# A two-expert-layer macaron block on one core: expert weights turned one at a time, 64-row keys, the subtraction of maxima between the two halves of the scores, key and query loads one per slot

## The chip, the cores and the metric

One core of a Trainium2 chip runs the whole block; the other cores are idle. The metric is the device time of one execution in microseconds (us). The kernel before takes 968.02 us, the median of three runs (967.27 to 972.53). The engines are named as in the profile: PE is TensorE (PEld its weight loads), DVE VectorE, ACT ScalarE, POOL GpSimd, SP SyncE.

## What is computed

The input is 16 sequences of 256 tokens with 128 features, 4096 tokens in all. The block is an expert layer, an attention layer, and the same expert layer again:

```
x = x + 0.5 * experts(layernorm(x))
x = x + attention(layernorm(x))
x = x + 0.5 * experts(layernorm(x))

experts:   scores = softmax(xf @ gate_w.T)                 # 8 experts
           vals, idx = top_k(scores.T, 512)                # each expert takes its 512 best tokens
           y   = layernorm(xf[idx]) * ln_w + ln_b
           h   = gelu(y @ fc1.T + b1)                      # 128 -> 512
           out = (h @ fc2.T + b2) * vals                   # 512 -> 128
           xf  = xf.at[idx].add(out)
attention: 16 heads of 8, causal, s[q,k] = (Q.K + Q.pek[k-q]) / sqrt(8)
           out = softmax(s) @ V + sum_k softmax(s) pev[k-q];  then @ Wo.T
```

All weights and activations are float32. The scores are computed with bfloat16 matmuls on float32 numbers split into three bfloat16 parts; six products of parts (TERMS) are kept, and stand as 48 rows of the contraction (6 terms times 8 features). The relative scores need a second set of 48 rows, so that a query operand has 96 rows, and 32 more for the causal mask.

## The kernel before

The program is written by hand, engine by engine, with semaphores.

**Expert layer** (`expert_layer(n)`, n = 0, 1). After gating and a bit search for the 512th score, PE and DVE work out the token numbers of each expert (`passed_of`, `index_of`, L884 to L897). POOL fetches each expert's rows with four indirect DMAs (`gather`, L543), adds each expert's output into the result in DRAM with four more (`scatter`, L554), and each scatter waits until the one before has landed. Five experts' rows (AHEAD) are fetched ahead; after the scatter of e comes the gather of e + 5. In layer 0 the scatters of experts 3 to 6 are each followed by two memsets (L570, L571), which clear rows 32 to 127 of the key buffers for the attention. PE first turns all 16 weight blocks of the eight experts (L913; ACT copies each from one of two PSUM banks, L700 and L702). Then for each expert it turns the fetched rows (`turn_rows`, L920), DVE scales them (`rows_in`, L1308), PE does the first matmuls (`first_half`, L929), ACT the gelu (L710), PE the second (`second_half`, L939), DVE scales the output (`scale`, L1296), POOL scatters. The second half of an expert stands behind the first half of the next one. The order of PE's loop is

```
turn all weights; turn_rows(0)
for e: first_half(e); turn_rows(e + 1); second_half(e - 1)      # the last two: second_half(e) as well
```

**Parts.** The attention starts with projections (L973) in 16 pieces of 512 tokens, queries and keys in turn. ACT takes the first part (L726) and the second (L730), DVE and POOL (L591, L594) the rests; SP stores every piece to DRAM (L440, `query_parts` 768 KB, `key_parts` 384 KB) from one of four buffers. From piece 4 on, SP issues one of the nine loads of the first pair behind each store (L447).

**Attention by pairs.** Two sequences are a pair; eight pairs follow each other, the six in the middle in a loop on every engine that is run three times with two pairs in it. A pair has 12 slots, and a slot makes 2 x 16 x 32 columns of scores in two halves (u = 0, 1). Each half has 16 matmuls with the relative table (L1002) and 16 with the keys (L1005, 128 rows of which 48 hold keys and the rest zeros). Between the halves PE turns the partial maxima of the slot before (L1017). After the second half it subtracts the maxima of the slot two back by 16 matmuls (`subtract_maxima`, L1025), which releases that slot's exponential on ACT (L778, 128 x 1024). Then comes a piece (`chunk`, L1056 or L1066) of the output products of earlier slots. Scores live in three pairs of banks, so the scores of slot s + 1 wait for the exponential of s - 2.

SP loads the operands of the next pair at the start of a pair: nine DMAs (`stacked`, L469), 384, 256 or 128 KB each, 2304 KB in all. The parts that a term needs are chosen by the tables Q_PART and K_PART: a query load reads one part and repeats it three times (or twice), a key load reads consecutive parts. Behind them in SP's queue stand the stores of the head outputs (L453, four small DMAs each) and of the relative outputs (L457).

## Time and profile before

| | us |
|---|---|
| median of three runs | 968.02 |
| the profiled execution | 967.66 |
| its span, first to last instruction | 965.9 |
| expert layer 0 | 0 to 228 |
| parts, until the first scores | 228 to 312 |
| attention by pairs | 312 to 715 |
| output projection, expert layer 1 | 715 to 965.9 |

Busy shares of the span: PE 66%, PEld 53%, DVE 52%, ACT 31%, POOL 24%. These are averages over stages with different limits. A row of the trace gives start and length in us (or a length alone), engine, line and operation, the tiles (almost everything lies in one tile, `arena`), and in brackets the idle time before with what ended it.

### The profile page before, as it was taken

The numbers are of one execution on the slowest core, as the hardware profiler recorded it, in microseconds if no ns is written. First come the engines' busy times: TensorE is split into PE (matmuls) and PEld (weight loads), VectorE is DVE, ScalarE is ACT, GpSimd is POOL, SyncE is SP. The second block draws the span as 40 slices with busy tenths as digits, with TensorE's granted clock in tenths as the row PEclk, the third lists the DMA queues.
The fourth block names the chain that finished last, engine by engine and source line by source line (L and its number), as shares of the span: only waits on it lengthen the run. The fifth ranks groups of instructions, "written<-read, shape, count | busy, mean of one in ns | idle before, by whom it ended". The sixth has DMA issues, their size and how long they took to land.

```text
span 965.9 us, 29195 instructions
## 1 busy us (share of the span) xinstructions
PE 636.5 (66%) x12366; PEld 516.7 (53%) x12366; DVE 504.7 (52%) x1712; ACT 297.2 (31%) x473; POOL 235.6 (24%) x227
## 2 busy tenths in 40 slices
PE   4512998700733789888898879899972811689640
PEld 3501556500422678777787768788862800357430
DVE  7977222123721567565666557667766777512120
ACT  2390454300522232323232313232332264063210
POOL 2000738884533000000000000014110000346864
PEclk9999999955885599999898979999985555599985
DMA  4272213325355332323222323234342506112322
GB/s 122 59 218 80 53 17 43 34 24 142 132 160 173 92 62 70 59 69 60 69 44 74 52 70 56 65 72 97 75 110 46 175 1 178 24 35 31 45 25 22
DMA packets 99163, 73.27 MB, mean 76 GB/s; under 512 B 26569, under 2 KB 92258, under 8 KB 98914
## 3 DMA queue, kind: packets, MB, share of 16 engines
q1 hardware_dynamic: 85858, 57.01, 23.4%
q0 software_dynamic: 13184, 14.43, 9.2%
q8 instruction: 102, 1.67, 0.8%
q14 instruction: 19, 0.16, 0.1%
HBM read 44.34 MB, written 27.01 MB: 74 GB/s over the span
## 4 chain that ended last, share of the span: by engine, by line
PE 38%; DVE 15%; POOL 14%; issue 11%; ACT 9%; SPq 6%; DMA 5%; DVEq 0%; ACTq 0%; POOLq 0%
PE banks L1002 10%; ACT arena L778 8%; PE banks L1005 7%; POOL x_mid L554 5%; PE banks L1025 5%; POOL out_dram L554 5%; SPq L469 3%; DVE arena L1119 3%; PE banks L1066 2%; PE banks L849 2%; POOL arena L543 2%; PE banks L929 2%; PE banks L913 1%; DMA out_dram<-arena 1%; SPq L440 1%
## 5 line engine op out<-in xcount | busy, mean ns | idle before, releaser
L778 ACT ACTIVATE arena<-banks 128x1024 f32<-128x1024 f32 x96 | 98.3, 1024 | 263.4 <-PE banks L1025 263.4
L1002 PE MATMUL banks<-arena 128*128 128x32 bf16 x3072 | 126.8, 194 | 42.8 <-issue 16.1
L1002 PEld LDWEIGHTS banks<-arena 128*128 128x128 bf16 x3072 | 112.4, 101 | 68.1 <-ACT arena L778 38.7
L1366 DVE TRANSPOSE_TENSOR_REDUCE arena<-banks 128x32 f32<-128x1024 f32 x96 | 120.0, 1250 | 18.1 <-PE banks L1005 13.8
L1005 PE MATMUL banks<-arena 128*128 128x32 bf16 x3072 | 108.6, 178 | 8.6 <-issue 8.6
L1005 PEld LDWEIGHTS banks<-arena 128*128 128x128 bf16 x3072 | 93.6, 97 | 11.3 <-issue 11.3
L543 POOL DMA_INDIRECT arena<-table,arena x64 | 61.5, 961 | 126.2 <-DVE arena L1276 107.7
L607 POOL COPY arena<-arena 128x576 f32 (+1 forms) x8 | 5.3, 668 | 329.6 <-PE banks L1056 329.6
L1382 DVE TENSOR_REDUCE arena<-banks 32x8 f32<-32x64 f32 (+1 forms) x96 | 20.1, 209 | 107.9 <-PE banks L1017 107.8
L710 ACT ACTIVATE arena<-banks,arena 128x512 f32<-128x512 f32 x64 | 44.0, 687 | 85.2 <-PE banks L929 85.2
L1025 PE MATMUL banks<-arena 128*128 128x64 bf16 x1536 | 64.4, 198 | 0.7 <-issue 0.7
L929 PE MATMUL banks<-arena 128*128 128x512 f32 x128 | 61.0, 609 | 3.6 <-DVE arena L1308 3.6
L939 PE MATMUL banks<-arena 128*128 128x128 f32 x512 | 61.8, 281 | 1.6 <-ACT arena L710 1.6
L939 PEld LDWEIGHTS banks<-arena 128*128 128x128 f32 x512 | 60.6, 198 | 3.2 <-ACT arena L710 3.2
L554 POOL DMA_INDIRECT out_dram<-arena x32 | 50.2, 1568 | 33.6 <-DVE arena L1296 15.1
L871 PE MATMUL banks<-arena 128*128 128x1 bf16 x60 | 11.2, 186 | 71.4 <-DVE arena L1228 71.4
L1066 PE MATMUL banks<-arena 128*32 128x128 f32 x1536 | 56.4, 288 | 1.4 <-issue 1.2
L554 POOL DMA_INDIRECT x_mid<-arena x32 | 50.2, 1570 | 24.2 <-DVE arena L1296 14.8
L1025 PEld LDWEIGHTS banks<-arena 128*128 128x128 bf16 x1536 | 54.5, 101 | 1.0 <-issue 1.0
L1056 PE MATMUL banks<-arena 128*9 128x128 f32 x1536 | 52.4, 278 | 3.5 <-ACT arena L785 1.9
L1293 DVE TENSOR_TENSOR arena<-banks,arena 128x512 f32<-128x512 f32 x16 | 11.1, 692 | 82.0 <-DMA x_mid<-arena 33.6
L1308 DVE TENSOR_SCALAR arena<-banks,arena 128x512 f32<-128x512 f32 x16 | 13.0, 810 | 73.1 <-PE banks L920 73.1
(182 smaller groups left out, 1021.4 us busy)
## 6 DMA issues: line engine op xcount, KB each, us to landing
query_parts<-arena SPq DMA_DIRECT2D x8, 768.0 KB, 6.4
arena<-query_parts SPq DMA_DIRECT2D x16, 384.0 KB
table<-arena SPq DMA_DIRECT2D x2, 2176.0 KB, 9.4
arena<-in_L_ffn_fc2s_dram SPq DMA_DIRECT2D x4, 1024.0 KB, 10.8
arena<-query_parts SPq DMA_DIRECT2D x16, 256.0 KB
key_parts<-arena SPq DMA_DIRECT2D x8, 384.0 KB, 7.0
arena<-key_parts SPq DMA_DIRECT2D x8, 384.0 KB
head_outputs<-arena SPq DMA_DIRECT2D x128, 18.0 KB
```

The lines of the kernel that those rows point to most:

```text
L543: pool.indirect_dma_start(out=rows[:, s, :], out_offset=None, in_=table[n], in_offset=bass.IndirectOffsetOnAxis(ap=idx[:, s:s + 1], axis=0 ...
L554: pool.indirect_dma_start(out=total[n], out_offset=bass.IndirectOffsetOnAxis(ap=idx[:, s:s + 1], axis=0), in_=osb[:, e % 2, j, :], in_offs ...
L710: nc.scalar.activation(hT[:, e % 2, c, :], psum[:, H_B[k % 2], :], ACT.Gelu_apprx_tanh, bias=b1T[:, e * NC + c:e * NC + c + 1]).then_inc(s ...
L778: nc.scalar.activation(dst, psum[:, 2 * r:2 * r + 2, :].rearrange("p u (h n) -> p u h n", h=H), ACT.Exp, scale=HD ** -0.5).then_inc(s_prob, 1)
L929: pe.matmul(psum[:, H_B[k % 2], :], w1T[:, e, P * c:P * c + P], yT[:, e % 2, :], start=True, stop=True).then_inc(s_h, 1)
L939: last = pe.matmul(o, hT[:, e % 2, c, P * j:P * j + P], w2T[:, e, c, :], start=(c == 0), stop=(c == NC - 1))
L1002: pe.matmul(sc[:, :, 2 * a:2 * a + 2], rel_k[:, y:y + P], q_st[:, r, :, q0 + 2 * a:q0 + 2 * a + 2], start=(a == 0), stop=False, skip_group ...
L1005: last = pe.matmul(sc[:, h], k_st[:, r, h, L * b + P * kb:L * b + P * kb + P], q_st[:, r, h, q0:q0 + 32], start=False, stop=False, skip_gr ...
L1025: last = pe.matmul(psum[:, 2 * (s % 3) + u, 64 * g:64 * g + 64], m_wts[:, s % 3, col:col + 1].to_broadcast([P, P]), eye2, start=False, sto ...
L1056: end = pe.matmul(psum[32 * j:32 * j + HD + 1, bank, P * u:P * u + P], v_pair[:, buffer, 2 * batch + kb, 4 * u + j, :], probs[:, blk, H * ...
L1066: end = pe.matmul(psum[32 * j:32 * j + 32, bank, P * u:P * u + P], rel_v[:, HD * x:HD * x + 32], probs[:, blk, :, q0:q0 + 4], start=(kb == ...
L1366: step(v.tensor_reduce(mp, psum[:, 2 * (s % 3):2 * (s % 3) + 2, :].rearrange("p u (h n) -> p (u h) n", n=32), AX.X, ALU.max, apply_transpo ...
```

## The change

- **Expert weights.** PE turns the two weight blocks of expert e + 1 between the first and the second half of expert e; only expert 0's come first. ACT copies them behind the gelu of e. The second half of e follows in the same step. DVE's loop is `rows_in(e + 1); scale(e)`. The copies that set the parity rows of the queries (eight, on ACT) come after the last expert.
- **POOL.** AHEAD is 4, and the memsets are gone.
- **Keys.** Their matmuls use rows 0 to 63. DVE clears rows 32 to 63 of the key buffers once, at the start of the attention (one memset of 32 x 8192 words).
- **Slot.** The subtraction of slot s - 2 stands between the halves of slot s.
- **Loads.** The terms are renumbered, so that query loads read consecutive parts too; key parts are stored in reverse order. The loads of the next pair are issued one per slot, each behind the wait for that slot's scores, among the stores. In the loop the parts are kept as the outer dimension of the access; only the first pair's loads fold parts and features into one by hand. In the program as built both are the same: the distance of two parts is that of 128 rows of 4096 elements, and the source is one dimension of 384 (256, 128) rows with such a step. Before, the repeated part had a step of 0 and stayed a dimension of 3 (or 2) of its own.

```diff
-        Q_PART = (0, 0, 0, 1, 1, 2)
-        K_PART = (0, 1, 2, 0, 1, 0)
+        Q_PART = (0, 1, 2, 0, 1, 0)
+        K_PART = (2, 1, 0, 1, 0, 0)
...
-                    q = qs[c, Q_PART[a], 0:HD, :, bass.ds(pr * PT, PT)]
-                    q = q.unsqueeze(0).to_broadcast([b - a, HD, H, PT])
-                    k = ks[0:b - a, :, :, bass.ds(pr * PT, PT)].rearrange("w d h n -> (w d) h n")
+                    q = qs[c, 0:b - a, :, :, bass.ds(pr * PT, PT)]
+                    k = ks[3 - (b - a):3, :, :, bass.ds(pr * PT, PT)]
+                    if spread:
+                        q, k = (x.rearrange("w d h n -> (w d) h n") for x in (q, k))
...
-                    elif not last:
-                        sp.wait_ge(s_score, NS * pr)
-                    if not last:
-                        for dst, src in stacked(pr + 1, 1 - r):
-                            sp.dma_start(dst, src).then_inc(s_load[1 - r], 16)
+                    loads = [] if last else list(stacked(pr + 1, 1 - r, False))
+
+                    def load_in(slots):
+                        for s in slots:
+                            if loads:
+                                sp.wait_ge(s_score, NS * pr + s + 1)
+                                sp.dma_start(*loads.pop(0)).then_inc(s_load[1 - r], 16)
+
+                    load_in((0, 1))
                     if not first:
                         store_heads(AV_LATER0, pr - 1, 2 * pr - 2, 1)
+                    load_in((2, 3, 4, 5, 6))
+                    if not first:
                         store_relative(pr - 1)
+                    load_in((7, 8))
+                    if not first:
                         store_heads(AV_LATER1, pr, 2 * pr - 1, 1)
...
-                AHEAD = 5
+                AHEAD = 4
...
-                    elif n == 0 and e < E - 1:
-                        q, i = 2 * H // 4, e - (E - AHEAD)
-                        pool.memset(k_words[32:64, q * i:q * i + q], 0.0).then_inc(s_zero, 1)
-                        pool.memset(k_words[64:P, q * i:q * i + q], 0.0).then_inc(s_zero, 1)
-                        pool.wait_ge(s_zero, 2 * i + 2)
...
+                def turn_weights(e):
+                    for w in range(2):
+                        if w and e:
+                            pe.wait_ge(s_yT, n * E + e)
+                        else:
+                            pe.wait_ge(s_trf, weights_read(n, 2 * e))
+                        bank = tr_bank(tr + NXB + 3 * e + w)
+                        for c in range(NC):
+                            src = raw2[:, e, P * c:P * c + P] if w else raw1[:, e, c, :]
+                            last = pe.transpose(bank[:, P * c:P * c + P], src, ident)
+                        last.then_inc(s_tr, 1)
...
+                turn_weights(0)
                 turn_rows(0)
                 for e in range(E):
                     first_half(e)
                     if e + 1 < E:
+                        turn_weights(e + 1)
                         turn_rows(e + 1)
-
-                    if 0 < e < E - 1:
-                        second_half(e - 1)
-                    if e >= E - 2:
-                        second_half(e)
+                    second_half(e)
...
-                            last = pe.matmul(sc[:, h], k_st[:, r, h, L * b + P * kb:L * b + P * kb + P],
-                                             q_st[:, r, h, q0:q0 + 32],
+                            last = pe.matmul(sc[:, h], k_st[0:64, r, h, L * b + P * kb:L * b + P * kb + P],
+                                             q_st[0:64, r, h, q0:q0 + 32],
...
+                        if u == 0 and between:
+                            subtract_maxima(s - 2, pr)
...
-                        if s >= 2 or not first:
-                            subtract_maxima(s - 2, pr)
...
+                dve.wait_ge(s_tab, 16)
+                v.memset(k_words[32:64], 0.0).then_inc(s_zero, 1)
```

PE's order at the start of an expert layer, before. L913 turns weights, L920 rows, L929 is a first half, L939 a second:

```order
L913 MATMUL banks<-arena 128x128 x64
L920 MATMUL banks<-arena 128x128 x4
L929 MATMUL banks<-arena 128x512 x4
L920 MATMUL banks<-arena 128x128 x4
L929 MATMUL banks<-arena 128x512 x4
L920 MATMUL banks<-arena 128x128 x4
L939 MATMUL banks<-arena 128x128 x16
```

The same place after the change. L926 turns weights, L934 rows, L943 is a first half, L953 a second:

```order
L926 MATMUL banks<-arena 128x128 x8
L934 MATMUL banks<-arena 128x128 x4
L943 MATMUL banks<-arena 128x512 x4
L926 MATMUL banks<-arena 128x128 x8
L934 MATMUL banks<-arena 128x128 x4
L953 MATMUL banks<-arena 128x128 x16
L943 MATMUL banks<-arena 128x512 x4
```

56 of 64 turns have moved behind the first half of expert 0, and its second half is ahead of the first half of expert 1.

PE in one slot of the loop, before (L1002 relative, L1005 keys, L1017 maxima turned, L1025 subtraction, L1066 chunk):

```order
L1002 MATMUL banks<-arena 128x16x2 x16
L1005 MATMUL banks<-arena 128x32 x16
L1014 REGISTER_ALU
L1017 MATMUL banks<-arena 32x128
L1002 MATMUL banks<-arena 128x16x2 x16
L1005 MATMUL banks<-arena 128x32 x16
L1025 MATMUL banks<-arena 128x64 x16
L1045 ISA
L1066 MATMUL banks<-arena 32x128 x16
```

The same slot after the change (L1014 relative, L1017 keys, L1031 maxima turned, L1039 subtraction, L1080 chunk):

```order
L1014 MATMUL banks<-arena 128x16x2 x16
L1017 MATMUL banks<-arena 128x32 x16
L1028 REGISTER_ALU
L1031 MATMUL banks<-arena 32x128
L1039 MATMUL banks<-arena 128x64 x16
L1014 MATMUL banks<-arena 128x16x2 x16
L1017 MATMUL banks<-arena 128x32 x16
L1059 REGISTER_ALU
L1080 MATMUL banks<-arena 32x128 x16
```

Half of the scores now stands behind the subtraction. Nothing was added or taken away in the slot.

## Rows read from the trace of the kernel before

**Rows 1.** The chain that ended last: start, length, scatters 0, 3, 7 of both layers.

```profile
136.24 1.64 POOL x_mid L554
...
174.12 1.63 POOL x_mid L554
...
218.72 1.56 POOL x_mid L554
...
873.37 1.63 POOL out_dram L554
...
911.23 1.63 POOL out_dram L554
...
950.14 1.55 POOL out_dram L554
```

**Rows 2.** PE's timeline at the start of expert layer 0.

```profile
107.49 3.35 PE L913 MATMUL banks<-arena 128*128 128x128 f32 x16
...
119.14 0.63 PE L920 MATMUL banks<-arena 128*128 128x128 f32 x4 [0.28 <-ACT arena L700]
120.67 3.89 PE L929 MATMUL banks<-arena 128*128 128x512 f32 x8 [0.90 <-DVE arena L1308]
...
130.06 3.74 PE L939 MATMUL banks<-arena 128*128 128x128 f32 x32
```

**Rows 3.** The waits: us in total, times, longest.

```profile
PEld banks L1002 <- ACT arena L778: 38.7, 81, 2.6
...
DVE arena L1119 <- DMA arena<-x_mid: 23.2, 1, 23.2
...
PE banks L1002 <- issue: 16.1, 6, 3.6
```

**Rows 4.** ACT's timeline while parts are made: pieces 0, 8 and 9.

```profile
246.73 0.58 ACT L726 CAST arena<-banks 128x512 bf16<-128x512 f32 x1 [1.12 <-PE banks L973]
...
265.75 0.58 ACT L726 CAST arena<-banks 128x512 bf16<-128x512 f32 x1 [0.22 <-DMA query_parts<-arena]
275.56 0.59 ACT L726 CAST arena<-banks 128x512 bf16<-128x512 f32 x1 [9.22 <-DMA key_parts<-arena]
```

**Rows 5.** PE's timeline: the first scores, and the scores of slot 4.

```profile
311.92 0.65 PE L1002 MATMUL banks<-arena 128*128 128x32 bf16 x16 [9.08 <-DMA arena<-query_parts]
...
326.99 0.67 PE L1002 MATMUL banks<-arena 128*128 128x32 bf16 x16 [1.11 <-ACT arena L778]
```

**Rows 6.** SP's timeline: loads of a pair.

```profile
504.72 0.83 SPq L469 DMA_DIRECT2D arena<-query_parts  x1
...
559.50 9.79 SPq L469 DMA_DIRECT2D arena<-query_parts  x2
```

**Rows 7.** Windows: length, busy of PE, PEld, DVE, ACT, POOL; clock, DMA share, GB/s.

```profile
286.00:292.00 6.00, 1.25 (x2) 0.30 (x2) 0.69 (x1) 2.20 (x5) 3.28 (x3) 0.65 0.97 236
...
370.00:376.00 6.00, 5.89 (x200) 5.50 (x200) 5.17 (x13) 1.52 (x2) 0.00 (x0) 1.00 0.35 89
```

**Rows 8.** The timeline of one slot of the loop.

```profile
521.64 0.66 PE L1002 MATMUL banks<-arena 128*128 128x32 bf16 x16 [0.19 <-ACT arena L778]
...
524.10 1.08 PE L1066 MATMUL banks<-arena 128*32 128x128 f32 x32
...
525.28 0.54 PEld L1002 LDWEIGHTS banks<-arena 128*128 128x128 bf16 x16 [0.37 <-ACT arena L778]
```

**Rows 9.** PE's timeline: a 128-row matmul, then two of 32 rows.

```profile
94.21 0.19 PE L895 MATMUL banks<-arena 128*128 128x1 bf16 x1
94.33 0.21 PE L897 MATMUL banks<-arena 32*128 32x1 bf16 x2
```

**Rows 10.** The chain again: an idle stretch of PE, and a chunk at the low clock.

```profile
511.70 3.07 issue
...
567.92 1.87 PE banks L1066 x32
```

**Rows 11.** Windows again, in expert layer 1: columns as in rows 7.

```profile
840.00:848.00 8.00, 8.00 (x56) 5.63 (x54) 1.95 (x6) 1.64 (x3) 6.17 (x7) 0.53 0.25 60
```

More of the change, by code:

```diff
@@ L327, in macaron_block, with stacked @@
         TAIL_BANK = (O_BANK, 0, 2, 3, 1)
-        def stacked(pr, r):
+        def stacked(pr, r, spread):
             for a, b in RUNS:
@@ L430, in attention @@
                 sp.dma_start(rel_v, bass.AP(pv_ext.tensor, 0, [[HD, P], [1, 2 * P * HD]])).then_inc(s_rv, 16)
-                loads = list(stacked(0, 0))
+                loads = list(stacked(0, 0, True))
                 for i in range(2 * NP):
@@ L711, in expert_layer @@
                                              bias=b1T[:, e * NC + c:e * NC + c + 1]).then_inc(s_g, 1)
-                    if n == 0:
-                        if e == 0:
-                            act.wait_ge(s_tr, tr + NAB)
-                            act.wait_ge(s_tab, 16)
-                            act.wait_ge(s_const, 9)
+                    if e + 1 < E:
+                        weights(e + 1)
+                if n == 0:
+                    act.wait_ge(s_tab, 16)
+                    act.wait_ge(s_const, 9)
+                    for e in range(E):
                         nc.scalar.copy(q_words[96:P, 4 * e:4 * e + 4],
@@ L986, in attention, with scores @@
                 pe.wait_ge(s_rv, 16)
-                pe.wait_ge(s_zero, 8)
+                pe.wait_ge(s_zero, 1)
                 pe.wait_ge(s_parity, E)
                 pe.wait_ge(s_eye, 1)
-                def scores(s, pr, r, turn):
+                def scores(s, pr, r, turn, between):
                     b, q, later = SLOTS[s]
@@ L1078, in pair @@
                     for s in range(NS):
-                        scores(s, pr, r, turn=s >= 1 or not first)
-                        if s >= 2 or not first:
-                            subtract_maxima(s - 2, pr)
+                        scores(s, pr, r, turn=s >= 1 or not first, between=s >= 2 or not first)
                         if s >= 8 or not first:
```

46 lines of the change are left out of this document (20 added, 26 removed).

## The prediction

> **What bounds the kernel now.** I read the chain that ended last first, then the waits, then the timelines of the places that it names. Three stages share the 965.9 us, each with a limit of its own.
>
> In the expert layers the chain is POOL's row of scatters [rows 1]. The first starts at 136.24 in layer 0 and at 873.37 in layer 1. Up to the fourth the pace is (174.12 - 136.24) / 3 = 12.63 us, since a gather follows each scatter. After it the pace is (950.14 - 911.23) / 4 = 9.73 in layer 1, scatter and landing alone, and (218.72 - 174.12) / 4 = 11.15 in layer 0, where memsets stand between. PE gets its say only before the first scatter: it turns weights from 107.49 and begins the first half of expert 0 at 120.67 [rows 2].
>
> While the parts are made, ACT waits for a buffer of parts to be stored: pieces 0 to 8 take 19.0 us, then piece 9 waits 9.22 us for a store [rows 4]. The scores start at 311.92 after 9.08 us of waiting for their loads [rows 5].
>
> In the pairs PE is nearly always busy. A steady slot takes 525.29 - 521.64 = 3.65 us, and its weight loads stand 0.37 us at its end for the exponential of three slots before [rows 8]. This wait totals 38.7 us over 81 times. Beside it stand idle stretches that nothing explains ("issue"): 16.1 us before L1002 [rows 3].
>
> **Expert layers, start: -11 us each.** From 107.49 to 119.14 PE turns 16 blocks, 0.73 us each [rows 2]. Now only two come first (1.5), then half a microsecond for ACT's copy, then the same 1.53 from rows to first half (120.67 - 119.14): the first half begins at 111.0 instead of 120.67. Its own work is 3.7; then two blocks and expert 1's rows, some 2.4, while ACT does the gelu; the second half of expert 0 starts at 117.1 instead of 130.06. From there to the scatter is 6.2 as before, so 123.3 instead of 136.24, 12.9 earlier. In layer 1 this stage begins at the low clock (0.53) [rows 11]. With less turning PE may do part of the first half at that clock, where a matmul of 512 columns takes up to twice as long. I charge 1.9, half of the worst, and take 11 (9 to 13). PE then needs 3.7 + 1.5 + 0.6 + 3.7, some 10 us an expert, under POOL's 12.6, so what hides the turned weights is POOL; without that cover they would cost 1.5 an expert.
>
> **Expert layers, pace: -3 us and +3 us.** With four ahead, four scatters are followed by a gather instead of three. Layer 0 was 3 x 12.63 + 4 x 11.15 = 82.5 from first scatter to last and becomes 4 x 12.63 + 3 x 9.73 = 79.7. Layer 1 was 3 x 12.63 + 4 x 9.73 = 76.8 and becomes 79.7 too. Together with the start: -13.8 and -8.1, **-22 us** (-18 to -26). DVE's new memset and ACT's eight copies fall into the 23.2 us in which DVE waits for the stored result to come back [rows 3]. DVE's clearing of 8192 words a row is not shown before; at the rate of the 512-column cast in rows 4, 0.58 us, it would take 9.3 us, and it fits. I charge nothing, and up to 2 us if that wait shrinks.
>
> **Parts and first loads: -14 us.** The trace shows what clogs the stores: nine loads of 2304 KB. In the window 286 to 292 the DMA engines moved 236 GB/s at a share of 0.97; while a pair's loads run, 370 to 376, they move 89 at 0.35 [rows 7], and SP stands in two query loads for 9.79 us [rows 6]. Such a load keeps few engines busy, and SP, full behind it, can't issue the next store. After the change the sources fold into one dimension and should spread. Then the pace of pieces 0 to 8, 19.0 / 8 = 2.4 us a piece, holds with little more: 2.6 for 15 pieces gives the last at 286, 5 us for its rests, and stores with loads (12 MB by then) at 236 GB/s need 50 us from 250, so about 298 instead of 311.92. I take -14; bounds -8 (the last five pieces still wait for stores) and -20.
>
> The Trainium skill ("DMA: Bandwidth & Descriptors", Rules for kernel authors) says why: a small outermost dimension, such as a leading repeat of c copies, confines a DMA to c engines. By that rule the trace agrees: three engines of 16 would be a share of 0.19, and rows 7 show 0.35 with the wide key loads among them.
>
> **First pair: -4 us.** Slots 3 to 7 have no chunk, and PE waits 1.11 us for each exponential [rows 5]. With the subtraction ahead of the second half, the exponential runs beside it. The turned maxima, which DVE must first reduce, become the next wait. Between nothing and all of 1.11 a slot goes; I take 0.8, since the exponential was the longer of the two paths: 5 x 0.8 = 4 (2 to 5).
>
> **Steady slots: -6 us.** The subtraction moves 0.9 us earlier, so ACT's exponential ends before the chunk does, and PE no longer waits for it. The gain per slot lies between 525.29 - (524.10 + 1.08) = 0.11, by the end of PE's work, and 0.37, by its weight loads [rows 8]; I take 0.25. Against it stands the change to 64 rows: twice a slot PE goes from a 128-row to a 64-row matmul. The nearest rows are those of 32: the first 32-row matmul starts 0.12 after the 128-row one [rows 9], where equal matmuls of a slot follow each other at 0.03 (16 weight loads busy 0.54 us [rows 8]). So one entry costs 0.09. The returns coincide with the turn and the chunk, which change the shape already. Per slot -0.25 + 2 x 0.09 = -0.07, over 88 slots -6. Bounds: -0.37 with free entries, -33; -0.11 with 0.18, +6.
>
> The skill ("TensorEngine Tiling (Array Packing)", Key Properties) says that changing the tiling mode drains the engine. By it each entry would expose a whole matmul, 0.19 [rows 9], less what runs on anyway: twice 0.16 a slot is 0.32 against 0.25, and this term would be +6 and the sum 12 higher.
>
> **Idle stretches and late stores: -12 us.** At 511.70 PE stands 3.07 us for nothing that the trace shows [rows 10]. That is 7 us after the first load of a pair, at 504.72 [rows 6], and the same place stalls in each turn of the loop, but not in the last pair, which has no loads. Two more such stretches stand behind each of the loop's two jumps back. I read them as instructions that come late behind the loads. One load per slot, spread over engines, should free those in the middle and shorten those at the jump; half of about 24 us (16.1 before L1002 and some 9 elsewhere). Bounds 0 and -17. The new waits of SP on each slot's scores have the stores behind them; a store waits for the slot's loads at most one slot longer than its data, and its buffer is read again three slots later. The last load goes out at the end of slot 8, with 3 slots, 10 us, to land. Nothing is charged.
>
> **Sum.** 967.66 - 22 - 14 - 4 - 6 - 12 = 909.7. The median of before is 0.4 above the profiled execution. I forecast **910 us**. The terms' own bounds give 967.7 - 26 - 20 - 5 - 33 - 17 = 867 and 967.7 - 18 - 8 - 2 + 6 - 0 = 946; all at one end is unlikely.
>
> **Rivals.**
>
> *Half-height matmuls keep the clock low.* This ends slower. PE's clock is at 0.53 in 840 to 848, where the index matmuls of 32 rows keep PE busy 8.00 of 8.00 us [rows 11]; dense 128-row work elsewhere is granted 1.00 [rows 7]. If matmuls that fill part of the rows don't raise it, the pairs run at 1.2 GHz instead of 2.4. A chunk then takes 1.87 instead of 1.08 [rows 8, 10], a subtraction of 64 columns twice its time (0.45 more), turn and transitions 0.2: 1.45 a slot, 88 slots, +128, so 1038. It decides from a clock below about 0.7 in the pairs. Against it: the relative half stays at 128 rows, and the slot becomes denser. Chance 0.07.
>
> *Half-height matmuls come at a slower beat.* If 64-row weights aren't loaded ahead, a key matmul comes every 0.05 us, as the two of 32 rows do (two take 0.21 together, 0.02 more than one of 0.19, and 0.05 from start to start at most [rows 9]), instead of 0.03: 32 x 0.02 = 0.65 a slot, 57 in all, 967. Against it: only the first pair after a switch is seen. Chance 0.05.
>
> *The loads still clog.* The rule of the skill named above speaks against the letter of the change: parts as the outer dimension would confine key loads as well. As mechanism of this kernel: two query loads, 640 KB, hold SP for 9.79 us [rows 6]; if the keys' loads run like them, a pair's 2304 KB take 35 us, which just fits into 12 slots of 3.6, 43 us. The idle stretches then stay (0 for 12) and the parts gain nothing (0 for 14): 936. The built program folds the dimensions, so 0.05.
>
> *PE, not POOL, paces the experts*, since the turned weights lie between the halves: 10 us warm, but up to 18 at the low clock. Eight times 5 us over POOL's pace in the worst layer: 950. PE is busy 80% and should stay warm. Chance 0.03.
>
> **How the numbers follow.** My forecast has 0.80. Its range is 884 to 942: two thirds of the way to the summed bounds on the low side, nearly all of it on the high side, where the clogging rival lies too. A measurement of this kernel tells 0.5%, 5 us, from no change. Faster by over that: forecast, clogging, most of the PE rival, 0.88; within it: the slower beat, 0.04; slower: the clock, and a slower beat combined with it, 0.08.
>
> **What the profile after should show.** The first scatter 11 us earlier in layer 0, scatters at 12.6 for four and 9.7 for three; the four-block rows of weights between the halves. The first scores at about 298 and no wait of 5 us or more for stored parts. In a slot the exponential starts inside the second half of scores, PE has no wait for ACT at L1014, and the slot takes 3.4 to 3.6 us. Query loads that occupy SP under 1.5 us each. The clock at 0.95 or more in the pairs. I am wrong if the key matmuls come slower than every 0.03 us, if the clock falls, if the stretches at the loop's middle stay, or if SP's per-slot waits make the stores late and the exponential waits for them.

## The result and the profile after

The changed kernel takes **920.53 us** (median of 4 runs, 916.85 to 921.84) beside 970.08 for the kernel before (4 runs on the same chip): a ratio of 0.9484, 95% interval 0.9441 to 0.9527. It is faster by 5.2%; 910 was forecast, with 884 to 942 as the range. Executions over 1.5% above the fastest of their kernel are left out of the medians and ratios below: one of four of the best version (893.16 with it) and two of four of folding alone (1018.86 with them). The profiled execution took 916.85, so 50.8 less than the 967.66 of before.

The page of the profile after (TensorE's share, its granted clock in 40 slices, the shares of the chain, and the weight loads of the relative score matmuls):

```profile
PE 655.4 (72%) x12366; PEld 533.6 (58%) x12366; DVE 509.4 (56%) x1713; ACT 294.8 (32%) x473; POOL 221.4 (24%) x219
...
PEclk9999999975975699998999899999985555579985
...
PE 51%; DVE 16%; POOL 14%; issue 10%; DMA 6%; ACT 2%; SPq 1%; DVEq 0%; POOLq 0%; ACTq 0%
...
L1014 PEld LDWEIGHTS banks<-arena 128*128 128x128 bf16 x3072 | 106.5, 101 | 36.7 <-issue 34.0
```

ACT and SP's queue have all but left the chain; PE carries the pairs. The weight loads of L1014 stood 38.7 us for ACT before [rows 3]; now 34.0 of their 36.7 idle us wait for nothing that the profile shows.

The chain that ended last (start, length; to be laid beside [rows 1] and [rows 10]):

```profile
123.22 1.63 POOL x_mid L566
...
173.82 1.62 POOL x_mid L566
...
202.78 1.55 POOL x_mid L566
...
417.27 3.12 issue
420.81 2.51 issue
...
819.42 1.64 POOL out_dram L566
...
869.95 1.63 POOL out_dram L566
```

Layer 0 scatters at 123.22 instead of 136.24. Four beats of (173.82 - 123.22) / 4 = 12.65 us follow, then three of (202.78 - 173.82) / 3 = 9.65; layer 1 begins with the same four, (869.95 - 819.42) / 4 = 12.63. Why the start moved stands in PE's timeline, beside [rows 2]:

```profile
107.47 1.97 PE L926 MATMUL banks<-arena 128*128 128x128 f32 x8
...
111.34 3.89 PE L943 MATMUL banks<-arena 128*128 128x512 f32 x8 [0.90 <-DVE arena L1320]
115.07 1.04 PE L926 MATMUL banks<-arena 128*128 128x128 f32 x8
```

Two blocks of weights are turned (the row's eight matmuls) in place of sixteen blocks, the first half of expert 0 starts at 111.34, and the next expert's weights are turned at 115.07, behind it.

The waits, over the whole span and then of PE from 276 to 670:

```profile
DVE arena L1131 <- DMA arena<-x_mid: 12.0, 1, 12.0
...
PE banks L1014 <- issue: 11.5, 4, 3.4
```

The first row is the wait for the stored result, 23.2 us before [rows 3]: DVE's clearing, 6.88 us at 196.03, now stands in it. The four waits for issue are the two pairs of stretches behind the loop's two jumps (417.27 and 420.81 above; the others at 515.5 and 519.3). Those in the middle of the loop are gone.

SP's timeline while parts are made:

```profile
252.55 1.13 SPq L451 DMA_DIRECT2D arena<-query_parts  x1
```

This is the longest load of the stage; the longest store takes 1.94. PE's and ACT's timeline of the first scores and of one steady slot (relative part, keys, turn, subtraction, relative part, exponential, keys, chunk, and the next slot):

```profile
277.56 0.65 PE L1014 MATMUL banks<-arena 128*128 128x32 bf16 x16 [3.20 <-DMA arena<-query_parts]
...
526.76 0.66 PE L1014 MATMUL banks<-arena 128*128 128x32 bf16 x16
...
527.35 0.56 PE L1017 MATMUL banks<-arena 64*128 64x32 bf16 x16
...
527.85 0.28 PE L1031 MATMUL banks<-arena 128*32 128x128 f32 x1
...
527.97 0.63 PE L1039 MATMUL banks<-arena 128*128 128x64 bf16 x16
...
528.43 0.65 PE L1014 MATMUL banks<-arena 128*128 128x32 bf16 x16
...
528.63 1.02 ACT L787 ACTIVATE arena<-banks 128x1024 f32<-128x1024 f32 x1 [3.63 <-PE banks L1039]
...
529.02 0.56 PE L1017 MATMUL banks<-arena 64*128 64x32 bf16 x16
...
529.51 1.08 PE L1080 MATMUL banks<-arena 128*32 128x128 f32 x32
...
530.52 0.66 PE L1014 MATMUL banks<-arena 128*128 128x32 bf16 x16
```

The first scores come at 277.56 instead of 311.92 [rows 5]. The exponential runs at 528.63, inside the second half of the scores, and is done before the chunk, as meant. But the slot takes 530.52 - 526.76 = **3.76 us, not less than the 3.65 of before** [rows 8].

The balance of the two profiled executions, from milestone to milestone:

| stretch | before | after | difference |
|---|---|---|---|
| to the first scatter, layer 0 | 136.24 | 123.22 | -13.0 |
| to DVE's first statistics after the reload | 95.6 | 92.6 | -3.0 |
| to the first scores | 80.1 | 61.7 | -18.4 |
| to the ninth turn of maxima | 35.8 | 36.6 | +0.7 |
| to the last turn (87 slots) | 356.6 | 348.1 | -8.5 |
| to the first scatter, layer 1 | 169.1 | 157.2 | -11.9 |
| to the end | 92.6 | 95.7 | +3.1 |

The 87 slots hide two opposite things. A slot is the time from one turn of maxima to the next. Their median length rose by 0.11 (+9 us), and what slots lasted beyond it (stalls and low clock; counted below as the **excess** of these 87 slots, over every slot more than 0.1 above the median) fell from 39.3 to 21.9 (-17 us). The +9 is what the table's -8.5 leaves beside -17; 87 x 0.11 alone would be +10.

### The profile page after: what moved, and what is told of

It is laid out like the page before. It is cut to its first block, busy times and chain, and to the rows that moved or that the text cites. A ratio compares the mean times of both kernels' runs of the same rounds, so it can differ in the third digit from the quotient of the medians.

```text
span 915.1 us, 29236 instructions
## 1 busy us (share of the span) xinstructions
PE 655.4 (72%) x12366; PEld 533.6 (58%) x12366; DVE 509.4 (56%) x1713; ACT 294.8 (32%) x473; POOL 221.4 (24%) x219
## 4 chain that ended last, share of the span: by engine, by line
PE 51%; DVE 16%; POOL 14%; issue 10%; DMA 6%; ACT 2%; SPq 1%; DVEq 0%; POOLq 0%; ACTq 0%
PE banks L1014 11%; PE banks L1017 10%; PE banks L1080 5%; PE banks L1039 5%; PE banks L1070 5%; POOL out_dram L566 5%; POOL x_mid L566 5%; DVE arena L1131 3%; POOL arena L555 3%; PE banks L1031 2%; PE banks L856 2%; DMA x_mid<-arena 1%; PE banks L878 1%; PE banks L891 1%; DVE arena L1157 1%
## 5 line engine op out<-in xcount | busy, mean ns | idle before, releaser
L1014 PE MATMUL banks<-arena 128*128 128x32 bf16 x3072 | 126.9, 194 | 16.6 <-issue 11.5
L1014 PEld LDWEIGHTS banks<-arena 128*128 128x128 bf16 x3072 | 106.5, 101 | 36.7 <-issue 34.0
L1017 PE MATMUL banks<-arena 64*128 64x32 bf16 x3072 | 109.7, 175 | 1.1 <-issue 0.9
L1017 PEld LDWEIGHTS banks<-arena 64*128 64x128 bf16 x3072 | 90.1, 94 | 11.2 <-issue 1.6
L1039 PE MATMUL banks<-arena 128*128 128x64 bf16 x1536 | 65.6, 198 | 1.2 <-issue 1.0
L1039 PEld LDWEIGHTS banks<-arena 128*128 128x128 bf16 x1536 | 63.3, 102 | 3.5 <-issue 1.7
L943 PE MATMUL banks<-arena 128*128 128x512 f32 x128 | 62.9, 626 | 1.8 <-DVE arena L1320 1.8
L953 PE MATMUL banks<-arena 128*128 128x128 f32 x512 | 62.7, 283 | 1.6 <-ACT arena L718 1.6
L953 PEld LDWEIGHTS banks<-arena 128*128 128x128 f32 x512 | 61.3, 200 | 3.2 <-ACT arena L718 3.2
L566 POOL DMA_INDIRECT x_mid<-arena x32 | 50.2, 1568 | 22.9 <-issue 8.5
L1080 PE MATMUL banks<-arena 128*32 128x128 f32 x1536 | 53.9, 284 | 0.3 <-issue 0.3
L878 PEld LDWEIGHTS banks<-arena 128*128 128x128 bf16 x60 | 6.3, 105 | 76.9 <-DVE arena L1240 76.9
## 6 DMA issues: line engine op xcount, KB each, us to landing
arena<-in_L_ffn_fc2s_dram SPq DMA_DIRECT2D x4, 1024.0 KB, 10.7
```

What stands on the lines that cost most here:

```text
L566: pool.indirect_dma_start(out=total[n], out_offset=bass.IndirectOffsetOnAxis(ap=idx[:, s:s + 1], axis=0), in_=osb[:, e % 2, j, :], in_offs ...
L943: pe.matmul(psum[:, H_B[k % 2], :], w1T[:, e, P * c:P * c + P], yT[:, e % 2, :], start=True, stop=True).then_inc(s_h, 1)
L953: last = pe.matmul(o, hT[:, e % 2, c, P * j:P * j + P], w2T[:, e, c, :], start=(c == 0), stop=(c == NC - 1))
L1014: pe.matmul(sc[:, :, 2 * a:2 * a + 2], rel_k[:, y:y + P], q_st[:, r, :, q0 + 2 * a:q0 + 2 * a + 2], start=(a == 0), stop=False, skip_group ...
L1017: last = pe.matmul(sc[:, h], k_st[0:64, r, h, L * b + P * kb:L * b + P * kb + P], q_st[0:64, r, h, q0:q0 + 32], start=False, stop=False, s ...
L1039: last = pe.matmul(psum[:, 2 * (s % 3) + u, 64 * g:64 * g + 64], m_wts[:, s % 3, col:col + 1].to_broadcast([P, P]), eye2, start=False, sto ...
```

## The experiments

Two theories stood against each other at the start. **Mine after the result**: the 64-row keys cost the steady slots what the order of the subtraction gives them, and the gain comes from the expert starts and from loads that are both folded and spread. **The rival**: the slot's new length is a price of the new order or of the loads between the slots, and the rows are free. Beside them: whether folding or spacing did the work on the loads. Medians below are of 4 runs each (10 for the repeated loads, 6 for the last one, 3 for the best version, 2 for folding alone), each beside the kernel before on its own chip.

**Keys of 128 rows in the changed kernel.** Rows 64 to 127 of the stored words have to be cleared then; GpSimd does it.

```diff
+                pool.memset(k_words[64:P], 0.0).then_inc(s_zero, 1)
+                pool.wait_ge(s_zero, 2)
...
-                            last = pe.matmul(sc[:, h], k_st[0:64, r, h, ...], q_st[0:64, r, h, q0:q0 + 32],
+                            last = pe.matmul(sc[:, h], k_st[:, r, h, ...], q_st[:, r, h, q0:q0 + 32],
```

> The changed kernel with the keys' matmuls at 128 rows again (POOL clears rows 64 to 127 of the key buffers in its idle time before the first parts); all else as changed. Theory (the 64-row form is what the slot pays for: 0.10 us more at each of two entries and 0.08 at the turn): the slot falls from 3.76 to about 3.45 us, 88 slots, and the run is 24 to 30 us faster than the changed kernel, about 890. Rival (the slot grew from 3.65 to 3.76 because the subtraction stands between the halves, or because DVE is late): the slot stays near 3.75 and the time near 920.

904.23 us, ratio 0.9354 (0.9304 to 0.9404), 16 less than the change; 24 to 30 were expected. PE's timeline of a slot:

```profile
522.94 0.66 PE L1016 MATMUL banks<-arena 128*128 128x32 bf16 x16
523.43 0.56 PE L1019 MATMUL banks<-arena 128*128 128x32 bf16 x16
523.84 0.27 PE L1033 MATMUL banks<-arena 128*32 128x128 f32 x1
...
524.41 0.66 PE L1016 MATMUL banks<-arena 128*128 128x32 bf16 x16
524.90 0.56 PE L1019 MATMUL banks<-arena 128*128 128x32 bf16 x16
525.39 1.08 PE L1082 MATMUL banks<-arena 128*32 128x128 f32 x32
526.40 0.66 PE L1016 MATMUL banks<-arena 128*128 128x32 bf16 x16
```

The slot is 526.40 - 522.94 = 3.46. Laid beside the slot above, three steps are shorter, each by about a tenth: relative part to keys 0.49 against 0.59, twice, and keys to turn 0.41 against 0.50. Keys to chunk is 0.49 in both. So the 64 rows cost at each entry and at the return before the turn, 0.3 a slot, and nothing at the return before the chunk. That is the 0.3 of the theory, 26 us over 88 slots. The run got less of it, since its excess rose from 21.9 to 36.0 and its pairs began late.

First scores at 285.26 instead of 277.56: two rows of its timeline say part of why, on GpSimd and on VectorE.

```profile
217.54 6.92 POOL L594 MEMSET arena<- 64x8192 f32 x1
```

```profile
220.05 4.43 DVE L1141 TENSOR_SCALAR arena<-arena 128x8 f32<-128x8 f32 x1
```

The eight values a row of L1141 take 0.17 us everywhere else; here the instruction ends when GpSimd's clearing does, at 224.5. The Trainium skill ("SBUF — State Buffer", "SBUF: two separate sides") says that VectorE and GpSimd share a pair of ports as an exclusive lock: of a GpSimd instruction and a VectorE one in a two-port mode, the one that starts first has the pair for its whole length, and the other waits. The two rows agree with it; in which mode L1141 ran no row shows.

**The subtraction behind the second half again**, 64 rows kept.

```diff
                         if u == 0 and turn:
                             turn_maxima(s - 1, pr)
-                        if u == 0 and between:
-                            subtract_maxima(s - 2, pr)
                     last.then_inc(s_score, 1)
+                    if between:
+                        subtract_maxima(s - 2, pr)
```

> The changed kernel with the subtraction behind the second half again, 64-row keys kept. Theory (order helps, rows hurt): PE waits for the exponential again, the slot is about 3.9 us, the run 8 to 18 us slower than the changed kernel, 928 to 938. Rival (the new order is what cost): the slot falls below 3.65 and the run is 8 or more faster.

940.84 us, ratio 0.9769 (0.9722 to 0.9817), 20 more than the change (8 to 18 were expected); the slot is 4.04 (3.9). PE's waits from 280 to 760 bring the exponential back:

```profile
PE banks L1014 <- ACT arena L787: 10.6, 19, 2.5
```

**The order alone, in the kernel before** (128 rows, repeated loads in a burst): the same edit the other way round.

> The kernel before with the subtraction of the maxima between the score halves alone (128-row keys, repeated loads in a burst, weights first). Theory (the exponential of the slot before gets its data in time, and TensorE's wait of 0.27 us ahead of the next slot's relative part goes): the slot from 3.65 to about 3.46, over some 90 slots -17, so 951 (948 to 956). Rival (the stretches behind the burst grow by what the slots give, since they are set by the transfers): 960 to 968.

955.21 us, ratio 0.9849 (0.9748 to 0.9951). The slot is 3.47, as the first theory had it. The excess rose from 39.3 to 50.4, so of the 16 us that the shorter slots save, 11 went back: as the rival said, if not to its full size. Of the 11, 5.5 are more waits for issue, and 4.3 is a wait of the second pair for its loads at 357.7, which the kernel before doesn't have. PE's waits from 316 to 700, to be laid beside the 16.1 us of [rows 3]:

```profile
PE banks L1002 <- issue: 20.2, 10, 3.9
PE banks L1005 <- issue: 10.9, 5, 3.2
```

With this run all four corners are there (medians of a slot; and, in brackets, from the first turn of maxima to the ninth):

| | 128 rows | 64 rows |
|---|---|---|
| subtraction behind the second half | 3.65 (32.2) | 4.04 (37.4) |
| subtraction between the halves | 3.47 (27.7) | 3.76 (32.6) |

The order gives 0.18 a slot at 128 rows and 0.28 at 64; the rows take 0.39 in the old order and 0.29 in the new. Both hold for the first pair too, where each is worth some 5 us. The corner of 128 rows and the new order is the kernel before with its repeated loads; the changed kernel with 128 rows has the same 3.47, and 28.2 in the first pair.

**All nine folded loads at the start of the pair**, in the changed kernel.

```diff
-                                sp.wait_ge(s_score, NS * pr + s + 1)
+                                reach(sp, s_score, NS * pr)
...
-                    load_in((0, 1))
+                    load_in(range(9))
```

> The changed kernel with all nine loads of the next pair at the start of a pair again, sources folded as changed. Theory (the spread over many engines freed instruction fetches and stores, not the spacing): 0 to 4 us slower than the changed kernel, about 921. Rival (one load per slot is what took the idle stretches of PE away): the stretches in the middle of the loop come back, 8 to 17 us slower.

999.03 us, ratio 1.037 (1.0298 to 1.0441): slower than the kernel before, the surprise of the study; neither theory had it. PE's waits from 280 to 760, and two windows of one pair (length, busy of PE, PEld, DVE, ACT, POOL, clock, DMA share, GB/s):

```profile
PE banks L1017 <- issue: 43.0, 6, 10.4
PE banks L1014 <- issue: 29.9, 7, 6.5
```

```profile
516.00:524.00 8.00, 7.44 (x226) 6.61 (x223) 6.17 (x15) 2.05 (x2) 0.00 (x0) 1.00 1.01 116
524.00:532.00 8.00, 1.49 (x42) 1.32 (x39) 1.54 (x6) 1.02 (x1) 0.00 (x0) 0.78 0.92 102
```

While the loads run the DMA engines are full (1.01, 0.92), all sixteen of them, and PE stands 10.36 us, until 535.85. The trace's packets of the instruction queue tell what it most likely stands for: code comes in packets of 16 KB, one every 4 us or so when PE is busy, and here one starts at 517.80 and the next only at 532.46 and ends at 534.04. The packets don't name the engine they are for; that they are PE's is inferred, since PE's matmuls and weight loads are 24732 of the changed kernel's 29236 recorded instructions, and since PE goes on behind the late packet. In the kernel before, a pair's loads filled 0.35 of the engines [rows 7], and the packet behind 504.22 came at 511.96 instead of some 4 us later: 3 us of delay, and 3.07 us of standing PE. So folding without spacing does harm; the idle stretches that I had halved for "spread over engines" are longer the wider a burst is.

**Folding alone, in the kernel before**, tells whether that needs anything of the changed kernel.

```diff
-        Q_PART = (0, 0, 0, 1, 1, 2)
-        K_PART = (0, 1, 2, 0, 1, 0)
+        Q_PART = (0, 1, 2, 0, 1, 0)
+        K_PART = (2, 1, 0, 1, 0, 0)
...
+                    q = qs[c, 0:b - a, :, :, bass.ds(pr * PT, PT)]
+                    k = ks[3 - (b - a):3, :, :, bass.ds(pr * PT, PT)]
+                    q, k = (x.rearrange("w d h n -> (w d) h n") for x in (q, k))
...
```

> The kernel before with the folded sources of the query and key loads alone (new tables of parts; all nine loads still at the start of a pair, 128-row keys, weights first, subtraction after the second half). Theory (each folded load fills all sixteen DMA engines with work, and nine of them one behind the other keep TensorE's instruction fetches waiting): the first scores about 18 earlier than 311.9, but stretches of issue of 5 to 10 us in every pair, as in the run of the changed kernel with the burst: 1000 to 1030. Rival (those stretches came from the burst meeting the slots of the changed kernel, and folding by itself is a gain): 940 to 955.

1009.77 us beside 967.81 for the kernel before, 42 more. The first scores are earlier by 17.1 (294.81), and PE's waits from 280 to 760 take it all back:

```profile
PE banks L1005 <- issue: 34.7, 6, 9.4
PE banks L1002 <- issue: 29.0, 5, 10.7
```

**Spacing alone**: the changed kernel with the old tables and repeated query loads, one per slot.

```diff
...
-                    q = qs[c, 0:b - a, :, :, bass.ds(pr * PT, PT)]
-                    k = ks[3 - (b - a):3, :, :, bass.ds(pr * PT, PT)]
...
+                    q = qs[c, Q_PART[a], 0:HD, :, bass.ds(pr * PT, PT)]
+                    q = q.unsqueeze(0).to_broadcast([b - a, HD, H, PT])
+                    k = ks[0:b - a, :, :, bass.ds(pr * PT, PT)].rearrange("w d h n -> (w d) h n")
...
```

> The changed kernel with the old tables of parts, so that query loads again read one part and repeat it; issue one per slot as changed. Theory (the repeat confines the query loads to few DMA engines and so holds up the stores of parts): the first scores come 15 to 20 us later, at about 295, the pairs lose 0 to 5, the run is 15 to 24 us slower, about 938. Rival (the parts came faster because of the earlier work alone, not the loads): within 3 us of the changed kernel.

970.83 us, ratio 1.0037 (1.0007 to 1.0068), 50 more than the change where 15 to 24 were expected. The first scores are back at 297.90, 20 later, as the theory had it, and the slots behind the ninth turn take 35 more: a wait stands in the pairs that neither kernel has. PE's waits from 280 to 760, and one of them in the timelines of SP (340 to 400), ACT and PE:

```profile
PE banks L1069 <- ACT arena L793: 22.6, 6, 4.7
```

```profile
376.08 6.04 SPq L474 DMA_DIRECT2D arena<-key_parts  x1
...
383.28 8.61 SPq L456 DMA_DIRECT2D head_outputs<-arena  x12
...
389.46 0.59 ACT L793 COPY arena<-banks 128x512 f32<-128x512 f32 x1 [6.08 <-DMA head_outputs<-arena]
...
390.09 1.90 PE L1069 MATMUL banks<-arena 128*9 128x128 f32 x32 [3.05 <-ACT arena L793]
```

A key load occupies SP for 6.04 us behind the repeated query loads (0.56 to 0.85 us a load in the pairs of the change), and the stores of the head outputs stand behind it on SP's queue. ACT can't read the next heads until their buffer is stored, and PE's chunk waits for ACT. This is close to the chain that the prediction feared from spacing (it had the exponential wait, not the chunk); with folded loads PE has no such wait. PE's waits for issue stay low, 14.6 us against 13.8 in the change and 26.7 before, so spacing by itself does take the stretches of the middle away.

**Three loads at a time**, behind slots 0, 3 and 6 of the changed kernel.

```diff
-                                sp.wait_ge(s_score, NS * pr + s + 1)
+                                sp.wait_ge(s_score, NS * pr + s // 3 * 3 + 1)
```

> The changed kernel with its nine folded loads issued three at a time, behind slots 0, 3 and 6. The same bytes and the same last slot but two. Theory (the length of the unbroken run of loads decides how long a fetch waits): between one per slot (920.5) and nine at once (999), each group of three giving stalls of 1 to 3 us where a fetch falls into it, 930 to 950. Rival (only a burst that outlasts TensorE's fetched instructions stalls it, and three loads don't): 917 to 925.

952.64 us, ratio 0.983 (0.9785 to 0.9874), between the two and just over what was expected; the excess is 61.4, between 21.9 for one and 97.8 for nine. PE's waits from 280 to 760:

```profile
PE banks L1017 <- issue: 16.3, 6, 3.7
```

Three loads, 1152 or 768 KB in the first two groups of a pair, are enough: beside the jumps the pairs have ten stretches of 1.6 to 3.7 us.

**The old order of the weights**, all sixteen banks turned first, in the changed kernel (on PE, ACT and DVE; PE's part):

```diff
-                turn_weights(0)
...
-                        turn_weights(e + 1)
+                for k in range(NWB):
+                    bank, e = bank_of(NXB + k), k // 2
...
+                    if 0 < e < E - 1:
+                        second_half(e - 1)
```

> The changed kernel with the old order of the expert layers alone: all sixteen weight banks turned before the first half of expert 0 (64-row keys, subtraction between the halves and folded loads stay). Theory (each layer starts later by the banks that stand ahead of its first half, and paces a little differently): the first scatter goes from 123.2 back to about 136.2, the reload's statistics from 215.9 to about 231.9, the layer after the pairs grows by about 9: +25, so 942 to 946. Rival (the new order only moved TensorE's cold stretch about, and the reload follows the stores of x_mid): the first scatter late by 13, but the end of the layer late by 5 or less: 926 to 930.

942.85 us, ratio 0.9706 (0.9629 to 0.9783), 22 more than the change. POOL's timeline has the first scatter at 136.71, and DVE's statistics start at 229.57, 13.7 later than in the changed kernel (16 were expected).

**Gathers five ahead.**

```diff
-                AHEAD = 4
+                AHEAD = 5
```

> The changed kernel with gathers five experts ahead instead of four. POOL has 6.8 us idle ahead of the first scatter, and one expert's gathers take 5.0; after it, gather and scatter share POOL at 12.6 us per expert for four experts, and then 9.6 us without gathers. Theory (POOL's queue paces the experts): the fifth gather fills the idle, one of the four 12.6 us beats becomes 9.6, so -3 per layer, 915 (913 to 917). Rival (the first scatter is late by the fifth gather, or the transfers pace it): within 1 of 920.5.

911.92 us, ratio 0.9397 (0.9325 to 0.9468), 1 below the range of the first theory. POOL's timeline shows the first scatter; the fifth expert's last gather starts at 120.47.

```profile
125.85 1.64 POOL L566 DMA_INDIRECT x_mid<-arena  x1 [4.44 <-DVE arena L1308]
```

The gathers fit into the idle time. From the first scatter to the statistics it takes 89.4 us instead of 92.6, and in layer 1 92.3 instead of 95.7 to the end: 3 us each. The first scatter, 2.6 later than the 123.22 above, isn't held by POOL; it stood at 124.8 to 125.3 in four other runs with four ahead, so the stage before it varies by that much. The profiled execution is 2.4 shorter than the change's; the median's further gain is more than this mechanism gives, and the intervals of the two ratios overlap.

**The version that beats both.** 128-row keys, five gathers ahead, and the clearing by VectorE, in the time in which it waits for the reload.

```diff
                 v.memset(k_words[32:64], 0.0).then_inc(s_zero, 1)
+                v.memset(k_words[64:P], 0.0).then_inc(s_zero, 1)
```

> The changed kernel with three edits: keys of all 128 rows again, rows 64 to 127 of the stored words cleared by VectorE in its idle time at the end of the expert layer (in the run of 128-row keys shown so far GpSimd did it, 6.92 us at 217.5, and the first statistics' subtraction on VectorE took 4.43 us in place of 0.17 meanwhile), gathers five experts ahead. Theory (the terms add up: the run with 128-row keys had 904.2; less 4 to 6 of the clearing, less 3 to 6 of the gathers): 895 (891 to 899). Rival (the clearing was hidden and the first scores are bound by the parts' loads): 899 to 903.

**890.34 us, ratio 0.9175 (0.9087 to 0.9263)**: 8.2% off the first kernel and 3.3% below the change (0.9175 against 0.9484). That is just under the theory's 891 to 899, so the terms add up. The trace is of the execution that took 898.84. DVE's timeline at the clearing and the reload:

```profile
203.47 6.88 DVE L1332 MEMSET arena<- 64x8192 f32 x1 [1.76 <-issue]
...
214.83 1.65 DVE L1131 BATCH_NORM_STATS2 arena<-arena 128x6 f32<-128x128 f32 x8 [3.55 <-DMA arena<-x_mid]
```

3.55 us of the wait are left, so the clearing is hidden. In this version the first pair shows something about the clock too. The windows from 298 to 314 of the change, and of this version, whose first scores come at 277.69 against 277.56 and whose slots differ in the rows of the key matmuls alone:

```profile
298.00:314.00 16.00, 14.85 (x350) 12.90 (x348) 8.64 (x24) 4.68 (x5) 0.67 (x1) 0.50 0.25 49
```

```profile
298.00:314.00 16.00, 14.44 (x455) 13.39 (x456) 11.00 (x30) 5.72 (x8) 0.67 (x1) 1.00 0.26 51
```

PE is busy for 14.85 and 14.44 us, but is granted 0.50, 1.2 GHz, with half its score matmuls on 64 rows, and 1.00, 2.4 GHz, with all on 128. With the subtraction between the halves this holds in every run: by the trace's clock records the low clock ends 34 to 44 us behind the first scores in the six runs with 64-row keys, 14 to 19 in the four with 128. In the old order it isn't as clear: 40 with 64 rows, but 27 in the kernel before and 38 with folding alone, where PE stands idle more in between.

**Each load one slot later** in that version, to keep the first slot behind a jump free.

```diff
-                                sp.wait_ge(s_score, NS * pr + s + 1)
+                                sp.wait_ge(s_score, NS * pr + s + 2)
```

> The version with 128-row keys, VectorE's clearing and five gathers ahead, with each of the nine folded loads issued one slot later (behind slots 1 to 9 in place of 0 to 8), so that none is issued in the first slot behind a loop's jump. In the trace of that version the two jumps cost TensorE 3.4 + 2.3 us and 3.4 + 2.5. Theory (a jump waits for two pieces of code one after the other, whatever the queues carry): the jumps keep their price and the time stays within 4 of 893. Rival (the load issued at the pair's start stands ahead of those pieces): the jumps fall to about half, and the time by 5 or more, 883 to 888.

914.18 us, ratio 0.9438 (0.9397 to 0.9478), 24 more: neither theory had that. The jumps kept their price (3.3 + 2.5 and 2.7 + 2.5 us), so the first was right about them, and all waits for issue together are the same, 22.9 us against 23.1. What is new is the chain of the repeated loads: PE waits 12.5 us for the copy of the heads, and not at all in the version before. The rest of the 24 is not taken apart; at each of the four waits over 2 us stand 3.4 to 6.8 us of low clock. PE's waits from 200 to 800, and the timeline of SP and PE:

```profile
PE banks L1070 <- ACT arena L794: 12.5, 6, 3.7
```

```profile
456.52 0.70 SPq L475 DMA_DIRECT2D arena<-query_parts  x1
457.46 7.99 SPq L457 DMA_DIRECT2D head_outputs<-arena  x12
...
463.66 1.90 PE L1070 MATMUL banks<-arena 128*9 128x128 f32 x32 [3.72 <-ACT arena L794]
```

The last load, now at the end of slot 9, goes out at 456.52, and the twelve stores of the head outputs stand behind it in program order. They are late by the slot that SP waited.

## Why the prediction was right, and where it was not

**Right**: the time, 1.1% off, inside the range; and the mechanisms for the starts and the parts, and that loads make the middle stretches. That the sum came so near is in part luck: errors of 20 us one way and some 12 the other all but cancelled.

**Expert starts, -11 each: -13.0 and -11.9.** The steps were met within 0.4: first half at 111.34 (111.0 predicted), scatter at 123.22 (123.3). The 1.9 that I charged for the cold clock wasn't needed in layer 0. With the pace, -3.0 and +3.1 for -3 and +3. Taken back, the order of the weights costs 22.

**Parts and first loads, -14: -18.4.** The loads occupy SP for 1.13 us at most, the longest store for 1.94, and the pieces wait 3.0 us at most for a store where one waited 9.22 [rows 4]. I kept a bound of 50 us for stores and loads together, at 236 GB/s; the window 234 to 277 took 43 at 246 GB/s, and PE waits only 3.20 for its loads. Folding alone gave 17.1 in the kernel before. The "about 298" for the first scores forgot that layer 0 ends 14 earlier: by my own terms it was 284, and 277.56 came.

**First pair, -4: +0.7.** The step itself was sound: at 128 rows the order gives 32.2 - 27.7 = 4.5. What failed is that nothing was charged for 64 rows here: they cost 4.5 to 5.2. Eight slots at 0.29 to 0.39 would be 2.3 to 3.1 of it; the rest goes with a low clock that lasts longer, and I have not separated the two. The rival that 64-row matmuls keep the clock low has a case for this stretch, at a price of 5 at most instead of 128; later in the pairs the clock is 1.00. The row that it was built on was read wrong: between the 32-row index matmuls stand 128-row ones (L895), and from 844.59 on PE turns weights with all 128 rows (L913).

**Steady slots, -6: +9. This is the step that failed.** My term was -0.25 for the order and 2 x 0.09 for entries. Measured at 128 rows the order gives 0.18 and not 0.25, and with the new order the rows cost 0.29 a slot and not 0.18: two entries at 0.10 and one return at 0.09. The sentence that failed is "The returns coincide with the turn and the chunk, which change the shape already". It holds for the chunk (0.49 in both runs) and not for the turn (0.50 against 0.41). The slower beat of key matmuls didn't come: 16 of them take 0.56 us at either height. The Trainium skill says that a change of tiling mode drains the engine ("TensorEngine Tiling (Array Packing)", Key Properties). The trace agrees in kind, with 0.10 us an entry; the prediction's estimate by that rule was 0.16, and nothing for the returns. The two terms, steady slots and first pair, came out 20 higher than mine.

**Idle stretches, -12: -17, for a reason half wrong.** By PE's waits for issue alone it is 26.7 before and 13.8 after, -13; the other 4 of the excess are slots that ran slow for other reasons, the low clock behind a stretch among them. I read the stretches as instructions that come late behind loads, and the burst's packets fit that. But I credited both halves of the edit, "one load per slot, spread over engines". Spreading over engines alone more than doubles the excess (39.3 before, 96.5 with folded loads); one load per slot is what removes the stretches, and only folded loads are short enough not to hold the stores. In the pairs neither half is worth anything without the other: folding without spacing costs 42 us in the kernel before and 78 in the changed one, spacing without folding loses 50 against the change, 35 of them in the steady slots and 20 ahead of the first scores.

**Late stores, nothing charged**: right for the change as written, but with less room than I said. One slot more of waiting on SP costs 24 us in the best version.

**The other rivals.** PE doesn't pace the experts: the beats of scatters are POOL's, 12.65 and 9.65. The loads don't clog. Both chances were small and stayed unused.

By sign: the wrong terms cost 15 and 5 us more than predicted, and the starts, the parts and the stretches gave 2 + 1, 4 and 5 more, so that the total came out 7 off on the profiled execution (8 by these rounded terms).

## What to carry to other kernels

Widening DMAs so that they use all engines made the packets of code wait behind the whole burst here, and TensorE with them: fold the source and space the issues, both or neither, and leave the queue's stores where their buffers need them. Matmuls of 32 columns on 64 rows between others on 128 saved nothing here (16 take 0.56 us at either height) and cost about 0.1 us at each change of height, but for the one that coincides with the chunk; count the changes in a loop, the way back too, before rows are cut. Where one change bundles several edits, ask of each what it does without the others: here the best version drops the 64 rows and takes back the fifth gather.

## What the hardware showed that I had not expected

- PE stands up to 10.7 us for code while nine folded loads (2304 KB) keep the sixteen DMA engines full; with three loads at once 1.6 to 3.7 us; with one per slot in the changed kernel little but 2.7 to 3.5 + 2.3 to 2.7 us at each jump, which issuing the loads a slot later did not change.
- A shorter slot makes more stretches of issue: 128 rows with the same loads raise the excess from 21.9 to 36.0, and the order alone in the kernel before from 39.3 to 50.4. By waits for issue alone it is 13.8 to 25.9, and 26.7 to 32.2. Perhaps PE then uses its code faster than it comes; I haven't tested this by itself.
- With 64-row matmuls in half of the scores the granted clock stayed at 1.2 GHz until 37.6 us behind the first scores, in the best version with 128 rows until 18.5.
- A clearing of 6.92 us by GpSimd stretched a VectorE instruction of 0.17 us to 4.43. VectorE's clearing takes the same 6.88, with 1.76 of issue in front of it, for 32 partitions (194.82 in the best version) and for 64 (203.47).
